# Eight chunks through one block: conv, normalisation and routing of a chunk placed between the expert units of the chunks ahead of it

## What is computed

```python
x = x + conv3x3(fake_quant_nvfp4(ln_channels(x)), fake_quant_nvfp4(conv_w))   # x: 32 x 64 x 16 x 16
t = tokens(x)                                                                # 16 x 16 pixels of an image are tokens
n = ln_tokens(t)                                                             # over the 64 channels
probs = softmax(n @ gate_w + gate_b)                                         # 8 experts; keep the two largest
for e in range(8):
    t_out += probs_kept[:, e] * (gelu(n @ W1[e] + b1[e]) @ W2[e] + b2[e])    # 64 -> 128 -> 64, all experts for all tokens
return from_tokens(t + t_out)
```

## Time and profile before

| | us |
|---|---|
| three runs | 200.63, 201.38, 202.51; median 201.38 |
| the profiled execution | 201.13 |
| its span, first to last instruction | 199.3 |

### The profile page before, as it was taken

How to read it: one execution, slowest core, us unless ns; L and a number is a source line. 1 busy time by engine, 2 the same in 40 slices (tenths; PEclk the granted TensorE clock), 3 DMA queues, 4 the chain that set the end, 5 groups by cost and what they waited for, 6 DMA issues and landing times.

```text
span 199.3 us, 3977 instructions
## 1 busy us (share of the span) xinstructions
PE 168.3 (84%) x1214; PEld 86.4 (43%) x1214; DVE 140.4 (70%) x451; ACT 116.6 (59%) x153; POOL 123.8 (62%) x117
## 2 busy tenths in 40 slices
PE   2986169899673497998999999999999999989990
PEld 2983135466362343543443443444443353345530
DVE  0899999999897988478576585684784494154452
ACT  2366803481378383459866776767766666646740
POOL 7699043998161350545877776677767477478582
PEclk9999859999999559999999999999999999999998
DMA  5980000000000049849659479379369548659701
GB/s 169 326 116 0 3 2 0 3 0 3 0 0 0 3 104 172 161 103 206 120 161 207 117 184 213 89 189 207 89 157 209 118 138 194 148 115 221 193 0 53
DMA packets 16320, 22.39 MB, mean 112 GB/s; under 512 B 2344, under 2 KB 8112, under 8 KB 16304
## 3 DMA queue, kind: packets, MB, share of 16 engines
q1 hardware_dynamic: 16144, 22.04, 49.1%
q10 hardware_dynamic: 160, 0.15, 0.3%
HBM read 19.82 MB, written 2.36 MB: 111 GB/s over the span
## 4 chain that ended last, share of the span: by engine, by line
PE 34%; DVE 26%; DMA 18%; ACT 8%; issue 6%; POOL 3%; SPq 3%; POOLq 1%; ACTq 0%; DVEq 0%
PE ps L1059 17%; PE ps L1076 14%; DMA gbc<-gate_rows 11%; DMA gate_rows<-gateT 5%; DVE xn L719 5%; DVE ssum L618 4%; POOL x L400 3%; SPq L278 2%; DVE xn L630 2%; DMA cw<-in_conv_w 2%; DVE gbc L701 2%; ACT xn L447 2%; PE ps L1015 1%; DVE gbc L706 1%; DVE gbc L711 1%
## 5 line engine op out<-in xcount | busy, mean ns | idle before, releaser
L400 POOL TENSOR_TENSOR x<-x,y_sb 128x512 f32 (+1 forms) x63 | 80.2, 1274 | 41.6 <-DVE y_sb L839 37.0
L546 ACT ACTIVATE work<-ps,bias_sb,w_back 128x1024 f32<-128x1024 f32 x64 | 77.0, 1204 | 39.0 <-PE ps L1059 38.9
L839 DVE SCALAR_TENSOR_TENSOR y_sb<-ps,bias_sb,gbc 128x512 f32<-128x512 f32 x64 | 47.5, 747 | 42.6 <-PE ps L1076 31.1
L1076 PE MATMUL ps<-work,w_sb 128*64 128x512 f32 x256 | 66.1, 594 | 2.5 <-ACT work L546 1.3
L1059 PE MATMUL ps<-xT,w_hi 128*64 128x512 f16 x256 | 40.0, 390 | 0.1
L1059 PE MATMUL ps<-xT,w_lo 128*64 128x512 f16 x256 | 39.6, 387 | 0.0
L1059 PEld LDWEIGHTS ps<-xT,w_hi 128*64 128x64 f16 x256 | 14.3, 111 | 31.7 <-issue 30.3
L1076 PEld LDWEIGHTS ps<-work,w_sb 128*64 128x64 f32 x256 | 18.3, 137 | 15.7 <-ACT work L546 4.6
L1059 PEld LDWEIGHTS ps<-xT,w_lo 128*64 128x64 f16 x256 | 15.6, 112 | 12.9 <-issue 1.0
L982 PE MATMUL ps<-qpad,cw_bd 128*128 128x512 bf16 x72 | 19.0, 411 | 1.7 <-POOL qpad L355 1.6
L379 POOL TENSOR_TENSOR hl<-xn,hl x8 | 9.2, 1157 | 15.8 <-DVE hl L762 9.0
(11 more groups left out here) (111 smaller groups left out, 173.9 us busy)
## 6 DMA issues: line engine op xcount, KB each, us to landing
gbc<-gate_rows SPq DMA_DIRECT2D x16, 768.0 KB, 9.5
gbc<-gate_rows SPq DMA_DIRECT2D x16, 256.0 KB, 4.0
x_sb<-in_x SPq DMA_DIRECT2D x8, 256.0 KB, 5.3
out<-x SPq DMA_DIRECT2D x8, 256.0 KB, 10.4
w_raw<-in_W SPq DMA_DIRECT2D x2, 256.0 KB, 6.2
w_sb<-in_W SPq DMA_DIRECT2D x1, 256.0 KB
gate_rows<-gateT SPq DMA_DIRECT2D x8, 32.0 KB, 3.4
cw<-in_conv_w ACTq DMA_DIRECT2D x2, 72.0 KB, 3.8
```

What stands on the lines that cost most here:

```text
L400: pool.tensor_tensor(x2[:, ds(c * W, W)], x2[:, ds(c * W, W)], y_sb[:, u % H_RING, :], ALU.add).then_inc(added, 1)
L546: act.activation(h_sb[:, u % H_RING, :], bank(H + 2 * (u % 2), 2 * W), ACT.Gelu, bias=b1_sb[:, u:u + 1], scale=w_back[:, u:u + 1]).then_in ...
L839: dve.scalar_tensor_tensor(y_sb[:, u % H_RING, :], bank(Y + u % 2), b2_sb[:, u:u + 1], gbc[:, slot, u, :], ALU.add, ALU.mult).then_inc(wei ...
L1076: last = pe.matmul(ps[r * CH:(r + 1) * CH, (Y + u % 2) * W:(Y + u % 2 + 1) * W], w2_sb[:, u, :], h_sb[:, u % H_RING, r * W:(r + 1) * W], s ...
```

## The change

The eight phases are gone as phases for chunks 2 to 7. The work is numbered by slots: in slot s PE issues the first product of unit s and the second product of unit s-2, DVE the weighing of unit s-2, POOL the addition of unit s-3, ACT the gelu of unit s. Chunks 0 and 1 are taken to their routing ahead of slot 0 (chunk 1's halves, chunk 0's gate transpose and chunk 2's conv come in slots 0 to 5 by hand). For chunks 3 to 7, and for chunk 2 from its halves on, each stage has a distance: a stage with distance d is issued in slot 8c - d, on each engine behind that slot's unit work, except on PE, where it is issued between the slot's first and second product (the transposes before quantising come behind the second product).

With it: every loop is written out; one PSUM bank (`S0`) serves the transposes before quantising and the centring, another (`S1`) conv, halves, logits and gates; hidden values have a buffer of their own; the second norm's root is a power on POOL (`inverse_root`) from chunk 2 on; exponentials are one instruction per chunk, each followed by a load of the gelu table; the low halves of the weights are made on POOL instead of DVE; the conv weights' copies are shared by ACT and DVE; ACT makes all high halves and copies of xT; the copy of the logits (`route_copy`) is gone; the gates come in four parts (eight DMAs a chunk instead of four).

```diff
-LOGIT_PARTS = ((0, 2), (2, 4), (4, 8))
-GATE_PARTS = ((0, 2), (2, 8))
-BY_POOL = NCH - 3
-XN_BY_DVE = NCH - 2
+LN1_PARTS = ((0, 3), (3, 8))
+LN1_DVE = 5
+ROOT_BY_ACT = 2
+GATE_PARTS = ((0, 2), (2, 4), (4, 6), (6, 8))
 UNITS = EXPERTS
+SLOTS = UNITS * NCH
 H_RING = 4
...
+
+TURN, BOUND, MAGN, BIASED, CONV, CENTRE, SUMS, NORM = 19, 18, 17, 16, 15, 13, 12, 11
+HALVES, TURNH, LOGITS, EXPS, TOPS, INDEX, GATES, TURNG = 10, 9, 8, 7, 7, 6, 5, 4
+
...
+        S0, S1, H, Y = 0, 1, 2, 6
+        SMALL = 2 * W
+        LAST_TAP, BT, WT, WB = SMALL, SMALL + CH, SMALL + 128, SMALL + 256
+        CENTRE_BANK = {0: 3, 1: 7}
...
+        def due(s, ahead, first=2):
+
+            c, rest = divmod(s + ahead, UNITS)
+            return c if rest == 0 and first <= c < NCH else None
 
...
+            def send_rows(c):
+
+                sp.wait_ge(gateT_ready, c + 1)
+                sp.dma_start(rows[c, :, :], gateT[:, :]).then_inc(rows_out, 16)
+
+            def spread_gates(c):
+
+                sp.wait_ge(rows_out, 16 * (c + 1))
+                if c == 0:
+                    sp.wait_ge(w_lo_ready, 1)
+                row = rows[c, :, :].rearrange("(e r t) n -> r e (t n)", e=EXPERTS, r=2)
                 for h, (first, last) in enumerate(GATE_PARTS):
+                    if c >= 2:
+                        sp.wait_ge(weighted, UNITS * (c - 2) + last)
                     for r in range(2):
-                        row = rows[ds(c, 1), :, :].rearrange("z (e r t) n -> (z r) e (t n)", e=EXPERTS, r=2)
-                        sp.dma_start(gbc[r * CH:(r + 1) * CH, slot, first:last, :],
-                                     row[r, first:last, :].partition_broadcast(CH)).then_inc(gbc_in[slot][h], 16)
+                        sp.dma_start(gbc[r * CH:(r + 1) * CH, c % 2, first:last, :],
+                                     row[r, first:last, :].partition_broadcast(CH)).then_inc(gbc_in[c % 2][h], 16)
 
             def store(c):
 
-                wait_alone(sp, (added, UNITS * (c + 1)))
-                sp.dma_start(out_d[:, ds(2 * c, 2), :],
-                             x2[:, ds(c * W, W)].rearrange("p (q n) -> p q n", n=PIX)).then_inc(out_stored, 16)
-
-            spread_gates(0, 0)
-            spread_gates(1, 1)
-            with sp.Fori(0, (NCH - 2) // 2) as i:
-                for s in range(2):
-                    spread_gates(2 * i + s + 2, s)
-                    store(2 * i + s)
+                sp.wait_ge(added, UNITS * (c + 1))
+                sp.dma_start(out_d[:, 2 * c:2 * c + 2, :],
+                             chunk(x2, c).rearrange("p (q n) -> p q n", n=PIX)).then_inc(out_stored, 16)
+
+            for c in range(NCH):
+                send_rows(c)
+                spread_gates(c)
+                if c >= 2:
+                    store(c - 2)
...
+            def inverse_root(c):
+
+                pool.wait_ge(ss2, c + 1)
+                link(pool.tensor_scalar(std2[:, c, :], ssum2[:, c, :], 1.0 / CH, LN2_EPS, ALU.mult, ALU.add))
+                pool.wait_ge(power_ready, 1)
+                pool.tensor_tensor(rstd2[:, c, :], std2[:, c, :], power[:, :], ALU.pow).then_inc(rstd2_by_pool, 1)
+
...
             quantised(0)
+            pool.wait_ge(w_hi_ready, 1)
+            by_expert = lambda t: t[:, 0:NW].rearrange("p (e h) -> p e h", e=EXPERTS)
+            pool.tensor_tensor(by_expert(w_scaled), by_expert(w_raw),
+                               w_inv[:, 0:EXPERTS].unsqueeze(2).to_broadcast([128, EXPERTS, HIDDEN]), ALU.mult)
+            link(pool.tensor_tensor(w_scaled[:, NW:], w_raw[:, NW:],
+                                    w_inv[:, EXPERTS:EXPERTS + 1].to_broadcast([128, EXPERTS]), ALU.mult))
             quantised(1)
+            pool.tensor_tensor(w_lo[:, :], w_scaled[:, :], w_hi[:, :], ALU.subtract).then_inc(w_lo_ready, 1)
+            low_half(0)
             quantised(2)
...
+            low_half(1)
+            residual(2)
+            inverse_root(2)
+
+            for s in range(1, SLOTS + 3):
+                if 3 <= s:
+                    add_unit(s - 3)
+                if s == SLOTS + 1:
+                    break
+                for ahead, stage in ((BIASED, quantised), (CONV - 1, residual), (SUMS, inverse_root),
+                                     (HALVES, low_half)):
+                    c = due(s, ahead, 2 if stage is low_half else 3)
+                    if c is not None:
+                        stage(c)
...
+            deviations1(1)
             take_v(1)
-            normalise(NCH - 2)
+            for c in range(LN1_DVE, NCH):
+                normalise1(c)
+            act.wait_ge(w_inv_ready, 1)
+            for e in range(EXPERTS + 1):
+                cols = slice(e * HIDDEN, min((e + 1) * HIDDEN, NW + EXPERTS))
+                last = act.activation(w_hi[:, cols], w_raw[:, cols], ACT.Copy, scale=w_inv[:, e:e + 1])
+            last.then_inc(w_hi_ready, 1)
+            square2(0)
+            deviations2(0)
             take_v(2)
-            normalise(NCH - 1)
...
             high_half(0)
+            square2(1)
+            deviations2(1)
+            take_xT(0)
...
+            load_table(ACT.Exp)
             high_half(1)
...
+            load_table(ACT.Gelu)
+            for s in range(SLOTS):
+                gelu(s)
+                if s == 0:
+                    take_xT(1)
+                if s == 2:
+                    take_gateT(0)
+                    take_conv(2)
+                if s == 3:
+                    square2(2)
+                if s == 3:
+                    exponentials(1)
+                    load_table(ACT.Gelu)
+                if s == 5:
+                    take_gateT(1)
+                for ahead, stage in ((TURN, take_v), (CONV, take_conv), (CENTRE, square2), (HALVES, high_half),
+                                     (TURNH, take_xT), (EXPS, exponentials), (TURNG, take_gateT)):
+                    c = due(s, ahead, 3 if stage in (take_v, take_conv, square2) else 2)
+                    if c is not None:
+                        stage(c)
+                        if stage is exponentials:
+                            load_table(ACT.Gelu)
...
+            reduce1(0)
+            upper_steps()
+            reduce1(1)
+            reduce1(2)
+            invert1(0)
+            normalise1(0)
+            normalise1(1)
+            normalise1(2)
+            reduce1(3)
+            bounds(0)
+            magics(0)
+            spread_conv_weights()
+            bias(0)
+            take_conv_weights()
+            weight_maxima()
+            for c in range(4, NCH):
+                reduce1(c)
+            weight_exponents()
+            bounds(1)
+            invert1(1)
+            magics(1)
+            residual(0)
+            bias(1)
+            weight_powers()
+            normalise1(3)
+            normalise1(4)
+            reduce2(0)
+            invert2(0)
+            residual(1)
+            normalise2(0)
+            bounds(2)
+            magics(2)
+            reduce2(1)
+            bias(2)
+            invert2(1)
+            normalise2(1)
             shifted_logits(0)
             settled()
...
+            route_max(0)
+            route_index(0)
             route_gates(0)
...
             shifted_logits(1)
...
             settled()
...
+            route_max(1)
+            route_index(1)
             route_gates(1)
...
+            reduce2(2)
+            normalise2(2)
+            for s in range(1, SLOTS + 2):
+                if s >= 2:
+                    weigh(s - 2)
+                for ahead, stage in ((BOUND, bounds), (MAGN, magics), (BIASED, bias), (SUMS, reduce2), (NORM, normalise2),
+                                     (LOGITS, shifted_logits), (TOPS, route_max), (INDEX, route_index),
+                                     (GATES, route_gates)):
+                    c = due(s, ahead, 3 if stage in (bounds, magics, bias, reduce2, normalise2) else 2)
+                    if c is not None:
+                        stage(c)
...
+            def turn_chunk(c):
+
+                if c < LN1_DVE:
+                    pe.wait_ge(xn1_by_dve, c + 1)
                 else:
-                    pe.wait_ge(xn1_late, c + 1 - XN_BY_DVE)
+                    pe.wait_ge(xn1_by_act, c + 1 - LN1_DVE)
+                if c > 0:
+                    pe.wait_ge(biased_ready, c)
+                if c > ROOT_BY_ACT:
...
+            def convolve(c):
+
+                pe.wait_ge(q_ready, c + 1)
+                if c == 1:
+                    pe.wait_ge(x2_by_dve, 1)
+                if c == 2:
+                    pe.wait_ge(gateT_ready, 1)
+                if c > 2:
+                    pe.wait_ge(z_ready, c)
+                for k in range(TAPS):
...
+            def turn_halves(c):
+
+                pe.wait_ge(xl_ready, c + 1)
...
+            def turn_gates(c):
+
+                pe.wait_ge(gate_ready, c + 1)
...
+            for c in range(6):
+                centre1(c)
             pe.wait_ge(const_ready, 5)
...
```

(45 more changed lines are left out.)

## The result

| | before | after |
|---|---|---|
| median, us (runs) | 201.94 (200.63 to 204.57, 4) | 278.25 (275.49 to 279.12, 4) |
| span and mean granted clock of the profiled execution | 199.3, 0.953 | 273.7, 0.882 |

The changed kernel takes 1.378 times as long, 95% interval 1.366 to 1.391. Its profiled execution (275.49 us) is the shortest of its four; the forecast's sum, 255.5 us of span, is held against that execution's 273.7.

What follows compares the result with a forecast made beforehand. PE was taken to bound the units, without room for added work. Start 52.6, slots 0 to 5 25.6, slots 6 to 45 135.3 and rest 42.0 gave span 255.5, with 1.83 around it 257 us; range 222 to 285.

Steps and rivals of the forecast that it cites:

- the mechanism of the waits: In the units, DVE stages stand behind the weighing, so PE waits for their results; 8.95 us per eight slots.
- the five places: PE waits per chunk: transposes before quantising 1.7, halves 1.7, conv 2.2, centring 1.3, gates 2.05 us.
- list of signs: First product at 47 to 56 us; in the units five PE waits a chunk, period 27 us, granted clock 1.00.
- start of the units: Front up to the first product of slot 0: at 52.6 us instead of 68.9.
- slots 0 to 5: First six slots, priced apart: 25.6 us, with the first weighing at 22.6 us.
- slots 6 to 45: Five periods of 27.4 us less a first wait of 1.7 that is absent: 135.3 us.
- the rest: Slots 46 to 52, eleven bare slots, two second products, last weighing and addition, and the end: 42.0 us.
- PE is at work two thirds of the time with gaps up to 2.2 us, so I expect full clock: PE's clock in the units: granted clock 1.00, so no time was added for half clock.
- The rival: PE's clock falls in the gaps; in half of the periods that is 46 us more, 303 us; chance 0.12.
- the serial piece: Front: ACT normalises three chunks and makes high weights; POOL scales them, then runs quantised(1), subtracting by 41.4 us.
- That everything hides: Units: stages are never late and PE is the bound; span 199.5, time 201.3 us, no change; chance 0.09.
- The rival that half of each wait is hidden: Units: 43 us of PE waits halved, for instance by shorter hand-offs; 236 us; chance 0.17.

Runs made afterwards that it cites:

- kernel with all stages first: Changed kernel with each slot's stages ahead of its unit work on DVE and POOL, and the high half ahead of the gelu on ACT; 224.57 us.
- kernel with quantised(1) early: Changed kernel with quantised(1) issued on POOL ahead of the wait for the high weights instead of behind it; 272.34 us.
- kernel with all orders changed: Kernel with all stages first, plus quantised(1) ahead of POOL's wait and early stages of chunks 1 and 2 rearranged; 212.73 us.
- filled kernel without the power: Changed kernel with six extra matmuls in each of two PE waits (conv, gates) and inverse_root's power replaced by a multiplication; 259.54 us.

## Why the prediction was right, and where its sum was off

It was right on the sign, on the mechanism of the waits and on the five places, and wrong on the clock. 257 was 21 us short of the median, and its 255.5 of span 18 short of the profiled one. By its own list of signs one failed: the clock was not 1.00 in the units, but 0.85 to 0.97. Nor is the size all skill: an early start (-2.75) hid a part of what the slots took more. By its terms:

| term | forecast | measured | difference |
|---|---|---|---|
| start of the units | 52.6 | 49.85 | -2.75 |
| slots 0 to 5 | 25.6 | 29.96 | +4.4 |
| slots 6 to 45 | 135.3 | 150.1 | +14.8 |
| the rest | 42.0 | 43.8 | +1.8 |

**The periods.** At full clock the changed kernel's periods would be 28.7 us (19.8 of PE work as in the kernel with all stages first, and waits of 29.35 - 20.48 = 8.9) and 25.3 for the last (19.1 and 6.2), 140.1 in all; the kernel with quantised(1) early has such a last period, 25.6 at clock 1.00. The other 10.0 are half clock: 12.0 us more of PE's work, less some 2 us by which the waits at L872 shrank in two periods, since half clock hid the power there. The forecast's step "PE is at work two thirds of the time with gaps up to 2.2 us, so I expect full clock" is the one that failed. It rested on a single window with little work and clock 1.00; such a window says what was granted in it, not what is granted behind it. The rival had the mechanism, but priced at half of the periods, 46 us, and that was too much: half clock covered a few us behind a wait seven times, and overlapped with waits, since DVE and POOL go on while PE is slow (as at L872). The remaining 4.8 are PE's work, 98.4 against 5 x 18.5 = 92.5, less 1.1 of waits. Conv was 2.1 for 2.0, centring 1.19 for 1.0, halves 0.65 for 0.5, logits 0.59 for 0.45, gates 0.33 for 0.25, transposes 0.56 for 0.55, read from start to start in the kernel with all stages first: a stage between two products starts about 0.1 late, and the second product behind it takes 0.05 more. I had counted the first for the halves alone. Together these are 0.9 us a period, 4.6 of the 5.9; the rest isn't assigned.

**The waits.** Halves 1.7 forecast, 1.3 measured; conv 2.2 and 2.1; centring 1.3 and 0.8; gates 2.05 and 2.0; transposes 1.7 and, at full clock, 2.6. The last was mis-sized by `inverse_root`, bounded at 1.27 and taken as nothing: it is 1.65, 0.92 of it exposed where the clock ahead of it was full. It was also thought to begin 0.9 us before PE ends slot 5's second product; it began when that ended (135.21, for 134.14 + 1.03). Conv's wait was right in size with the wrong name. `quantised` and the release of the bank end within 0.1 us of each other, and the latter is last because DVE's L738, a 128 x 64 subtraction, takes 0.95 us instead of the 0.22 that it takes at 50.53, where POOL is idle: in the timeline of the changed kernel, first DVE, then POOL,

```profile
119.36 0.95 DVE L738 TENSOR_TENSOR ex<-logit,lmax 128x64 f32<-128x64 f32 x1
```

```profile
118.96 1.27 POOL L351 TENSOR_TENSOR qpad<-work,xn 128x512 bf16<-128x512 f32 x1 [1.31 <-DVE work L723]
```

it ends with POOL's subtraction. The Trainium skill (SBUF — State Buffer, SBUF: two separate sides) says that a DVE instruction with two SBUF inputs and a GpSimd instruction that reads SBUF exclude each other for their whole length; the trace agrees.

**Slots 0 to 5.** The first weighing was put 22.6 us behind the start, and stands there: 72.47 - 49.85 = 22.6. PE's second product, which waits for it, shows 5.6 us idle:

```profile
73.35 1.97 PE L971 MATMUL ps<-h_sb,w_sb 128*64 128x512 f32 x4 [5.59 <-DVE y_sb L778]
75.08 1.09 PE L957 MATMUL ps<-xT,w_hi 128*64 128x512 f16 x4
```

Behind it PE is at half clock from 73.35 to 79.22, nearly to slot 6, and the last stretch takes 7.3 us (72.47 to 79.81) where the forecast had 3.0. At full clock those 5.87 us would be some 2.9 less (an estimate, half of them): the same step failed here, and some 1.4 of the 4.3 have another cause, which wasn't looked for.

**The start** was 2.75 early because the high weights were ready at 35.6, not 37.3, and their scaling on POOL took 1.9 instead of 2.7; the serial piece itself, `quantised(1)` behind the wait for them, was there.

**The rest** was 1.8 longer: 35.2 us of PE's work where the forecast had 33.8, and 8.6 idle where it had 8.2, with the 1.3 for the gelu at slot 52 among them.

**The other rivals.** That everything hides fell with the waits. Its arithmetic, PE's work as the floor, is what the kernel with all orders changed ran into: 211.2 of span, where the rival said 199.5 with a start at 52.6. Its start is 8.2 us earlier than that, but from there on PE works 152.8 us instead of 142.5 and idles 13.9 instead of 4.4. The rival that half of each wait is hidden (236) fell too: at full clock the waits would be 41.8 of the 42.8 us forecast.

**Open.** What a wait has to be for the clock to fall isn't settled, only that in the periods of these traces it fell in or behind waits of 2.0 to 2.7 us, not behind each of them, and never where the longest was 1.6 or less. Whether a shorter front, or slots 0 to 5 at full clock, could pay for the PE work wasn't tried.

## What to carry to other kernels

Work moved onto the engine that sets the end must be paid there in full, and what it frees elsewhere counts only by what the critical chain there gives up; compare the two per item before anything is moved. If stages are interleaved with a steady loop, put each slot's stage ahead of the slot's own loop work on every engine that isn't the bound: the distance of one slot is lost when it stands behind. And where an engine's clock depends on what it did before, don't judge two edits that shorten its waits one at a time.

## What the runs showed of the hardware

- GpSimd's power of 128 x 8 elements: 1.65 us; a multiplication in its place 0.20; an addition of 128 x 512 1.26 to 1.31.
- The clock fell to half in or behind waits of 2.0 to 2.7 us, and stayed at 1.00 in the filled kernel without the power, with 4.9 us of waiting a period in five waits, none over 1.6. The Trainium skill (TensorE: Matmul & The Clock Gate, A second HAM failure mode: psum-queue depth-cycling) tells of a kernel in which frequent short idle times made the clock swing between its two levels. The changed kernel's seven pieces at half clock agree with that; the filled kernel without the power, idle five times a period and at 1.00 in all of them, shows that frequent idle times alone need not do it.
- Four of the five executions of that kernel, whose profiled one has the clock at 1.00 in all periods, lie within 0.35 us of each other (the fifth is 1.5 above), those of the changed kernel 3.6 us apart.
